# Three attention layers of a graph network: the order of VectorE's and TensorE's work at the start of a batch

## The reference, cut to what matters

```python
def _gat_layer(x, src, dst, W, a_src, a_dst, b):
    N = x.shape[0]
    H, C = a_src.shape
    h = (x @ W).reshape(N, H, C)
    alpha_s = jnp.einsum('nhc,hc->nh', h, a_src)
    alpha_d = jnp.einsum('nhc,hc->nh', h, a_dst)
    e = jax.nn.leaky_relu(alpha_s[src] + alpha_d[dst], NEG_SLOPE)
    m = jax.ops.segment_max(e, dst, num_segments=N)
    m = jnp.where(jnp.isfinite(m), m, 0.0)
    ex = jnp.exp(e - m[dst])
    den = jax.ops.segment_sum(ex, dst, num_segments=N)
    alpha = ex / (den[dst] + 1e-16)
    msg = h[src] * alpha[:, :, None]
    out = jax.ops.segment_sum(msg, dst, num_segments=N)
    return out.reshape(N, H * C) + b
...
for l in range(W.shape[0]):
    x = jax.nn.relu(_gat_layer(x, src, dst, W[l], att_src[l], att_dst[l], bias[l]))
```

## Time and profile before

| | us |
|---|---|
| median of 3 runs | 16749.57 |
| lowest and highest of them | 16744.98, 16754.85 |
| the profiled execution, its own time | 16653.95 |
| its span in the trace | 16652.1 |
| mean granted TensorE clock in it | 0.593 |

### The profile page before, as it was taken

One profiled execution on the slowest core, in us unless ns is written; L12 is line 12 of the kernel. 1 busy time (PEld: TensorE's weight loads), 2 busy tenths in 40 slices (PEclk: granted clock), 3 DMA queues, 4 the chain that ended last, 5 costly groups with the idle time before them and its releaser, 6 DMA issues. The chain is left out here.

```text
span 16652.1 us, 181011 instructions
## 1 busy us (share of the span) xinstructions
PE 6317.3 (38%) x36108; PEld 5357.2 (32%) x36109; DVE 5208.7 (31%) x16216; ACT 4100.0 (25%) x10462; POOL 8151.6 (49%) x8448
## 2 busy tenths in 40 slices
PE   0100005784444434799433333333333333333333
PEld 0000005762332322577432332323223233322332
DVE  6200003422222222322433333343333334333334
ACT  0000005702333333100222222222222222222222
POOL 2777771003555555100355555545555554555554
PEclk7555555586566666699655555555555555555555
DMA  6000002361221112377222222212222222222221
GB/s 210 11 11 9 9 9 63 81 202 34 39 39 38 39 38 39 95 223 222 82 50 50 52 51 51 51 46 51 50 51 51 51 48 49 51 50 52 52 51 46
DMA packets 1157570, 1039.16 MB, mean 62 GB/s; under 512 B 707670, under 2 KB 822582, under 8 KB 1157072
## 3 DMA queue, kind: packets, MB, share of 16 engines
q1 hardware_dynamic: 809536, 614.67, 13.3%
q0 software_dynamic: 265824, 340.03, 10.2%
q10 hardware_dynamic: 81744, 80.28, 1.5%
HBM read 940.04 MB, written 95.72 MB: 62 GB/s over the span
## 5 line engine op out<-in xcount | busy, mean ns | idle before, releaser
L525 POOL DMA_INDIRECT sb_G<-attention_table,sb_NOW x4992 | 4747.6, 951 | 3530.2 <-issue 1460.3
L860 PE MATMUL sums<-sb_G,sb_HOT 128*128 128x100 f32 (+2 forms) x16640 | 3443.1, 394 | 2724.0 <-ACT sb_HOT L651 1248.0
L860 PEld LDWEIGHTS sums<-sb_G,sb_HOT 128*128 128x128 f32 x16640 | 3285.0, 303 | 3012.0 <-issue 2756.1
L525 POOL DMA_INDIRECT sb_G<-feature_table,sb_NOW x1664 | 1573.9, 946 | 1330.8 <-DVE sb_NOW L1432 817.6
L1878 DVE TENSOR_TENSOR sb_ACC<-sb_ACC,sums 128x100 f32 x4992 | 1280.3, 256 | 2825.4 <-issue 1239.5
L582 POOL DMA_INDIRECT edge_counts<-sb_G x1625 | 1734.0, 1067 | 805.8 <-issue 535.3
L1418 DVE TENSOR_TENSOR sb_ACC<-sb_ACC,sums 128x97 f32 (+1 forms) x3328 | 849.9, 255 | 3956.5 <-remote 2447.7
L647 ACT ACTIVATE sb_H<-sb_iota_row,sb_H 128x128 f32<-128x128 f32 x4992 | 1528.7, 389 | 134.3 <-issue 45.5
L647 ACT ACTIVATE sb_HOT<-sb_iota_row,sb_HOT 128x128 f32<-128x128 f32 x3328 | 1015.4, 389 | 2008.8 <-remote 1381.1
L706 ACT ACTIVATE psC<-sb_SB 128x128 f32<-128x128 f32 x156 | 43.8, 281 | 5839.2 <-DVE sb_SB L1831 4863.5
L1037 PE MATMUL psD<-sb_lone,sb_HOT 1*128 1x4 f32 x312 | 90.7, 359 | 2213.3 <-DVE sb_lone L1838 1713.5
(11 more groups left out here) (435 smaller groups left out, 8993.4 us busy)
## 6 DMA issues: line engine op xcount, KB each, us to landing
sb_G<-edge_counts SPq DMA_DIRECT2D x1152, 256.0 KB, 3.3
sb_H<-rel_rows SPq DMA_DIRECT2D x624, 256.0 KB
sb_G<-in_edge_attr_dram SPq DMA_DIRECT2D x1664, 48.0 KB
sb_G<-attention_table,sb_NOW POOLq DMA_INDIRECT x4992
edge_counts<-sb_LW ACTq DMA_DIRECT2D x12, 6272.0 KB, 42.5
sb_EA<-in_edge_attr_dram SPq DMA_DIRECT2D x1664, 16.0 KB
sb_G<-feature_table,sb_NOW POOLq DMA_INDIRECT x1664
edge_counts<-sb_G POOLq DMA_INDIRECT x1625
```

The source lines that it names most:

```text
L525: pool.indirect_dma_start(to, None, rows, bass.IndirectOffsetOnAxis(ap=index, axis=0)).then_inc(landed, 16)
L860: last = nc.tensor.matmul(bank[:, k // 4, k % 4 * width:(k % 4 + 1) * width], HOT[:, hot, k, :], G[:, slot, k, 0:width], start=True, stop= ...
```

## The change

Only the order of instructions on VectorE and TensorE changes.

VectorE: `tail` gets two helpers. Behind L1835 (the shared node's exponent) it now builds the next batch's transposed one-hots 0 and 1, then waits for the exponential and asks, then weighs groups 0 and 1, and only then waits for the reply and corrects the shared node. Behind it stand weigh 2, one addition, weigh 3, the one-hots 2 and 3, and only now `sources`; head holds no one-hots any more.

TensorE: the next batch's logits 0 and 1 stand ahead of the reply for the shared node; logits 2 stand behind sums 1, logits 3 behind sums 2 and so ahead of sums 3. The four replies keep their places among the sums, except that logits no longer stand between them.

```diff
@@ -1061,20 +1061,20 @@
+                    logits_next(0)
+                    logits_next(1)
                     pe.wait_ge(SEM["hot_built"], 8 * it + (t2.base["hot_built"] + BG * half + 1))
                     reply(it, half, HEAD_ASKS)
                     add_edges(0)
                     add_edges(1)
-                    logits_next(0)
+                    logits_next(2)
                     reply_next(0)
                     add_edges(2)
-                    logits_next(1)
+                    logits_next(3)
                     reply_next(1)
                     reply_next(2)
                     add_edges(3)
-                    logits_next(2)
                     reply_next(3)
-                    logits_next(3)
@@ -1807,7 +1807,7 @@
-                def tail(it, half):
+                def tail(it, half, turn, weigh):
@@ -1834,8 +1834,12 @@
                     v.tensor_scalar(worth, worth, JOIN[:, ds(batch_no, 1)], None, ALU.mult)\
                      .then_inc(SEM["exponent"], 1)
+                    turn(0)
+                    turn(1)
                     dve.wait_ge(SEM["exp_made"], 4 * it + (t.base["exp_made"] + 2 * half + 2))
                     ask_lane(v.tensor_scalar(worth, worth, -1.0, None, ALU.add))
+                    weigh(BG * half)
+                    weigh(BG * half + 1)
                     reply()
@@ -1880,23 +1884,23 @@
                 def batch(it, half, more=True, last=False):
-                    tail(it, half)
-                    if not last:
-
-                        sources(it + 1, half)
+                    def turn(q):
+                        if more:
+                            turned(it, BG * (half + 1) + q)
+                    tail(it, half, turn, weigh)
                     adds = Adds(it, half)
 
-                    weigh(BG * half)
-                    weigh(BG * half + 1)
                     weigh(BG * half + 2)
                     adds(1)
                     weigh(BG * half + 3)
-                    if more:
-                        turned(it, BG * (half + 1))
-                        turned(it, BG * (half + 1) + 1)
+                    turn(2)
+                    turn(3)
+                    if not last:
+
+                        sources(it + 1, half)
                     adds(7)
                     if more:
-                        head(it + half, 1 - half, adds, lambda q: turned(it, BG * (half + 1) + q))
+                        head(it + half, 1 - half, adds, lambda q: None)
                     adds(BT - adds.tile)
```

## The result

| | median us | runs |
|---|---|---|
| before | 16750.93 (16744.98 to 16754.85) | 4 |
| after | 17438.31 (17402.69 to 17465.47) | 4 |

The ratio is 1.0409, 95% interval 1.0389 to 1.043: the change costs 687 us, 8.9 us in each of 77 pairs of batches. The forecast was 16640 with a range up to 17200, so both sign and size are missed. The profiled execution of after has a span of 17448.4 us.

The account below looks back on a forecast made before the run. Bound: a closed loop of tail, sums 0, gathers, head, with TensorE's results late during gather runs. Even half +4.0 and odd half −5.4 give −1.4 us a pair, times 77, −110: 16,640 us; own range 16,560 to 16,750, whole range up to 17,200.

Parts of the forecast that it names:

- The reading of the bottleneck: While GpSimd issues a long run of gathers, TensorE's results reach others late, until about 3 us behind the run.
- The way from tail to the first gather, +3.0 us: Each batch: first gather 13.45 us behind L1817 instead of 10.45, mostly because sources stands later; costs 3.0 us.
- The second danger: Tail behind the even half: the shared node's reply, now later in a gather run, may be held until 10.6 us.
- The extreme of 15.8: Upper end for that tail: with the reply held, first gather 15.8 us behind L1817, a cost of 5.4 us.
- the 5.2 us: VectorE's work from the shared node's reply to the first gather: scaling, weighings 2 and 3, addition, one-hots, sources, hop.
- The gain of the odd half, −5.4 us: Logits 2 and 3 ahead of sums 3 free tail; first gather to next first gather 52.3 us instead of 57.7.
- In the even half the rest of the loop, 38.2, is kept: Even half: the 38.2 us from first gather to next tail stay unchanged; L1817 waits only for its own queue.
- 36.2 behind the first gather: Odd half: tail begins when VectorE's additions end, 36.2 us behind the first gather instead of 47.3.
- Rival 2: Faster: GpSimd's 3.8 us pause between gather runs vanishes, −2.8 us a batch, −430 us, 16,320; chance 0.12.
- Rival 1: Slower: odd half's 11 us wait moves to a held reply 3, or VectorE crawls; +355 us, 17,105; chance 0.38.
- The crawl of VectorE: Rival 1's second form: 709 ns register instructions in tail inside the run use up the 11 us; chance 0.19.
- The rule of the Trainium skill on the shared port pair: VectorE and GpSimd lock a shared port; one-hots leaving gather runs save at most 38 us, not in the sum.

Follow-up runs that it names:

- e4: The kernel before, with one more GpSimd wait: for all four logits, ahead of a batch's fourth group of gathers; 16110.12 us, ratio 0.9672 on a late chip.
- e1: The changed kernel, with one more GpSimd wait: for the batch in front's reply 1, ahead of the third group's gathers; 16526.29 us, ratio 0.9923, late chip.
- f1: The changed kernel itself, unaltered, measured against before on a prompt chip, where TensorE's results aren't late; 12602.98 us, ratio 0.9987.
- g2: The kernel before, with only TensorE's logits 2 and 3 moved ahead of sums 3, on a late chip; 16355.14 us against 16722.35, ratio 0.9782.
- h1: The changed kernel, with TensorE's reply 1 moved ahead of the next batch's logits 3, on a late chip; 16631.49 us, ratio 1.0023 to before.
- e3: The changed kernel, with TensorE's logits 0 and 1 back behind sums 1, 2 behind sums 3, 3 behind reply 3; 16506.4 us, ratio 0.991 to before.
- h2: The kernel before, with GpSimd's four-logits wait and weighings 0 and 1 ahead of the shared node's reply wait, late chip; 15936.46 us, ratio 0.9607.

## Why the prediction was wrong, point by point

**The reading of the bottleneck** (results late in a run of gathers) was right as far as it went: e4 and e1 gain and f1 has none of it. Beside it the 709 ns of a register instruction were put aside as not decisive and as belonging to the even half's first run. They are in the odd half's first run too (L1876 between 12077 and 12096: up to 1384 ns), and in g2 they decide when the gathers begin.

**The way from tail to the first gather, +3.0 us.** Predicted 13.45, measured 13.9 and 13.6 in the two batches of after above. The second danger came true in part, the reply for the shared node held in the run: L1844 waited 4.10 us in one batch, 410.2 us in 104 in all. The extreme of 15.8 wasn't reached in it. That number was added up a little high as well: the parts of the 5.2 us sum to 5.1, and the run of eight from 12059.25 ends 7.3 behind tail, so 3 us more are 10.3 and not 10.6.

**The gain of the odd half, −5.4 us.** The logits moved ahead of sums 3 do bring tail forward, and the size is near where that is made alone: in g2 it is 53.3 us from first gather to first gather, forecast 52.3, before 57.7. But what gave part of it back wasn't the named step. The reply for the shared node was to be held to the end of the run; it came at once, and VectorE's slow register instructions took the time. The run ended at 12115.58 and L1847 began 2.2 us later, so both end shortly behind the run, and the near size is in part luck. In the changed kernel the wait ahead of L1817 did go, but the late reply 1 took its place.

**"In the even half the rest of the loop, 38.2, is kept", and tail "36.2 behind the first gather" in the odd half.** These are the steps that failed. From the first gather to the next tail it took 12605.23 − 12562.98 = 42.3 us in the even half and 12549.41 − 12502.47 = 46.9 in the odd one. VectorE waited for reply 1 in both, 26.6 us each time; before, it was there 3.3 us behind a run of 16. Some 3 us of the odd half's 11 couldn't go at all: even in g2 VectorE stands 2.95 us ahead of L1817 there with nothing to wait for. With the longer way that makes 55.8 and 60.9: +7.1 where the forecast had +4.0, and +3.2 where it had −5.4. I carried parts of the loop over as lengths, while they are sequences of hand-overs whose moments depend on where the pauses fall. The late `sources` had moved the gathers against reply 0 and sums 2, and so the pause was gone and reply 1 late.

**Rival 2, "the pause between runs goes: −2.8 a batch".** Its condition came true, its price had the wrong sign. I counted the pause as 3.8 us of GpSimd's time. In this order of TensorE's, with sums 2 and logits 3 ahead of reply 1, it was the moment at which reply 1 was handed over; h1 and e3 show that another order does without it. My own first paragraph says so: results come about 3 us behind the run. I applied it to logits and to the shared node's reply, and not to reply 1, which lies in the run that grew from 16 to 24 gathers.

**Rival 1**, the slower one, gave the right side for the wrong reason: reply 3 was not held (g2), and the wait ahead of L1817 did go, as forecast. The crawl of VectorE is real in g2 (5.0 us a pair), but in the changed kernel it isn't what costs: its two tails above reach the first gather at 13.9 and 13.6 us, and the time goes in the wait for reply 1.

**The rule of the Trainium skill on the shared port pair** gave at most 38 us from one-hots that leave the runs. A gather's mean went from 951 to 947 ns, 0.004 × 4992 = 20 us of GpSimd's. That agrees in sign; it can't be seen in the time, and no run moves the one-hots alone.

## What to carry to other kernels

Before a move shortens or removes a pause, ask what else is delivered in it: an idle stretch of one engine may be the window in which another's results arrive. When latency depends on the state of another engine, don't carry a part of a loop over as a fixed length; list the hand-overs and place each anew. And where results are late in the order in which they are made, the one that the critical chain needs stands first.

## What the runs showed of the hardware

Whether TensorE's results are late while GpSimd issues gathers depends on the chip: the kernel before takes 16587 to 16751 us in four comparisons and 12617 to 12639 us in four others, by the same instructions; a gather takes 951 ns on the late kind (before) and 950 on the prompt one (f1). The register instructions of VectorE that take 0.7 us while gathers are issued are found on the late kind alone. The orders of work differ by 8% between the fastest (h2) and the slowest (the changed kernel) on the late kind; on the prompt kind these two and all others measured there agree with before within 0.2%. The kernels of e1 to e4 weren't measured there. What makes a chip the one or the other isn't shown by any run. A wait that GpSimd doesn't need for its data can speed up a kernel on the late kind by 3.3% (e4), by giving the others a gap in its issue.
